# Summing part of a softmax denominator with an adding DMA instead of matmuls, and spacing out a row scatter

## The reference, cut to what matters

```
x = x + relu(normalised(adj + I) @ (layernorm(x) @ W.T))          # graph stage
h = layernorm(x)
q, k, v = projections of rmsnorm(h) with rotary positions          # 4 query heads, 2 key heads, 32 channels each
att = softmax(causal(q @ k.T / sqrt(32)))                          # over 8192 positions
h = h + (att @ v) @ wo.T
out = sum over the 2 best of 8 experts of  weight * (silu(f @ w1.T) * (f @ w3.T)) @ w2.T,  f = rmsnorm(h)
x = x + h + out
```

## Time and profile before

| | us |
|---|---|
| median of 3 runs | 4111.01 (4106.96 to 4114.44) |
| the profiled execution, its own time | 4112.9 |
| its span | 4111.2 |
| attention stage in it: first to last exponential | 1496.2 to 3666.8 |

### The profile page before, as it was taken

One profiled execution on the slowest core, in us unless ns is written; L12 is line 12 of the kernel. 1 busy time (PEld: TensorE's weight loads), 2 busy tenths in 40 slices (PEclk: granted clock), 3 DMA queues, 4 the chain that ended last, 5 costly groups with the idle time before them and its releaser, 6 DMA issues. The chain is left out here.

```text
span 4111.2 us, 48117 instructions
## 1 busy us (share of the span) xinstructions
PE 3444.4 (84%) x16381; PEld 1321.4 (32%) x16381; DVE 2755.8 (67%) x3882; ACT 1306.3 (32%) x1635; POOL 1641.3 (40%) x1016
## 2 busy tenths in 40 slices
PE   1456899999999959988899899999889999965990
PEld 1233444444444422222222222222222222213650
DVE  7877887704444447777878877777777776515773
ACT  0000000000000013443454355454445455634660
POOL 1000000000000014544675496565558566873564
PEclk8567889999999969999999999999899999987995
DMA  9888998788887526500000000000000000002226
GB/s 377 345 344 345 348 336 328 290 300 303 285 298 282 206 101 243 209 10 4 26 19 6 5 24 13 10 1 10 1 17 15 6 1 6 6 16 85 72 69 210
DMA packets 165282, 572.71 MB, mean 139 GB/s; under 512 B 20193, under 2 KB 55786, under 8 KB 114550
## 3 DMA queue, kind: packets, MB, share of 16 engines
q1 hardware_dynamic: 91304, 457.35, 29.8%
q10 hardware_dynamic: 60432, 88.88, 6.1%
q0 software_dynamic: 13360, 24.03, 1.8%
HBM read 478.22 MB, written 90.57 MB: 138 GB/s over the span
## 5 line engine op out<-in xcount | busy, mean ns | idle before, releaser
L958 DVE TENSOR_REDUCE unit_max<-ps_max 128x1 f32<-128x512 f32 (+3 forms) x2176 | 1356.3, 662 | 422.8 <-PE ps_max L1215 306.7
L786 POOL TENSOR_TENSOR chunk_sum<-chunk_sum,probs 128x1024 f32<-128x1024 f32 (+1 forms) x528 | 1194.8, 2263 | 570.2 <-ACT probs L918 556.1
L918 ACT ACTIVATE probs<-ps_scores 128x1024 f32<-128x1024 f32 (+1 forms) x1088 | 1021.1, 984 | 1048.3 <-PE ps_scores L1234 858.8
L1215 PE MATMUL ps_max<-keep_k_stack,q_stack 96*128 96x512 f16 (+3 forms) x2176 | 762.7, 383 | 154.0 <-DVE unit_max L958 113.9
L1234 PE MATMUL ps_scores<-q_stack,keep_k_stack 97*128 97x512 f16 (+3 forms) x2176 | 617.3, 379 | 38.6 <-ACT probs L918 34.7
L1245 PE MATMUL ps_out<-probs,keep_v 128*32 128x512 f32 (+3 forms) x4352 | 567.1, 593 | 0.6 <-ACT probs L918 0.6
L314 DVE TENSOR_TENSOR partial_degree<-partial_degree,ring 128x2048 f32<-128x2048 f32 x240 | 550.0, 2292 | 7.1
L1215 PEld LDWEIGHTS ps_max<-keep_k_stack,q_stack 96*128 96x128 f16 x2176 | 182.1, 97 | 972.3 <-DVE unit_max L958 822.1
L497 PE MATMUL ps_gather<-ring,keep_attended 128*128 128x512 f32 x960 | 448.2, 629 | 22.1 <-DVE keep_attended L338 22.1
L512 PE MATMUL ps_gather_low<-ring,keep_attended 128*128 128x512 f32 x800 | 360.6, 607 | 1.4 <-DVE keep_attended L338 1.4
L277 POOL DMA_DIRECT2D scratch_lower<-lower x15 | 9.3, 618 | 815.3 <-ACT lower L416 815.3
(11 more groups left out here) (232 smaller groups left out, 2712.2 us busy)
## 6 DMA issues: line engine op xcount, KB each, us to landing
ring<-in_adj SPq DMA_DIRECT2D x392, 1024.0 KB, 7.0
scratch_slots<-empty_rows ACTq DMA_DIRECT2D x16, 2080.0 KB, 7.4
scratch_parts<-empty_part ACTq DMA_DIRECT2D x8, 2048.0 KB, 7.7
moe_parts<-scratch_parts SPq DMA_DIRECT2D x64, 256.0 KB, 4.8
moe_x_rows<-scratch_slots SPq DMA_DIRECT2D x39, 260.0 KB
x_in<-in_x SPq DMA_DIRECT2D x16, 256.0 KB, 7.0
x_in<-in_x ACTq DMA_DIRECT2D x16, 256.0 KB, 9.8
cos<-in_cos ACTq DMA_DIRECT2D x16, 256.0 KB, 7.2
```

What stands on the lines that cost most here:

```text
L786: nc.gpsimd.tensor_tensor(chunk_sum[:, :, lo:], chunk_sum[:, :, lo:], weights, ALU.add).then_inc(chunk_added, 1)
L918: nc.scalar.activation(probs[:, j, kv, :, lo:], ps_scores[kv][:, :, lo:], ACT.Exp, scale=SCALE).then_inc(exp_done, 1)
L958: nc.vector.tensor_reduce(unit_max[:, i, at:at + 1], bank[:, 0:width], AX_X, ALU.max).then_inc(bank_free, 1)
L1215: last = nc.tensor.matmul(out[:, 0:width], q_stack[0:SHIFT_ROW, T % QBUF, h, s * P:(s + 1) * P], k_stack[0:SHIFT_ROW, h // NREP, G * BT:G ...
```

## The change

In the units with 1 <= v < T (105 of the 136), key head 1 of chunks 0 and 1 is no longer summed by PE. After adding chunk 1 of key head 0, POOL issues one DMA over `probs[:, 0:2, 1]` (128 partitions x 2 chunks x 1024 float32, 1 MB) into a new SBUF tile `unit_sums` of that shape: a plain copy in the first such unit of a block, an adding DMA (`accum_op=ADD`) in the others. ACT waits for that DMA before it overwrites key head 1 of chunks 0 and 1 in the next unit. Once per block with T > 1, in the last chunk of unit v = T, PE contracts `unit_sums` with the ones, as `add_weights` does. Without the pair after j = 1, PE keeps the gap order of the even chunks in chunk 1. Separately, `scattering` spreads the scatters (and the copies on ACT that go with them) of the batches with pace 2, the first three, over every second chunk: 16 units instead of 8.

```diff
+    first_added = {}
+    for T in range(NB):
+        for v in range(1, T):
+            first_added[first_unit(T) + v] = v == 1
+    added_before = lambda unit: sum(1 for other in first_added if other < unit)
...
         for b, start in enumerate(scattered_at):
-            n = (unit - start) * SUB + j
-            if 0 <= n < len(batches[b]) * SUB * TOPK:
+            n, late = divmod((unit - start) * SUB + j, paces[b])
+            if 0 <= n < len(batches[b]) * SUB * TOPK and not late:
                 yield b, n
...
+        unit_sums = sb("unit_sums", [P, 2, NREP, BT])
...
+            def add_pair(T, unit):
+
+                pool.wait_ge(exp_done, unit * EXPS + PER_CHUNK * 2)
+                if added_before(unit):
+                    pool.wait_ge(pair_added, 16 * added_before(unit))
+                out, src = (tile.rearrange("p c r t -> p c (r t)") for tile in (unit_sums[:], probs[:, 0:2, 1]))
+                if first_added[unit]:
+                    if T > 2:
+                        pool.wait_ge(unit_sums_used, T - 2)
+                    pool.dma_start(out, src).then_inc(pair_added, 16)
+                else:
+                    pool.dma_start(out, src, accum_op=ALU.add).then_inc(pair_added, 16)
...
                         add_chunk(T, first_unit(T) + n, j, n == 0)
+                        if first_unit(T) + n in first_added and j == 1:
+                            add_pair(T, first_unit(T) + n)
                         route(first_unit(T) + n, j)
...
                         if kv == 0:
                             act.wait_ge(chunk_added, unit * SUB + (j - SUB + 1))
+                        elif unit - 1 in first_added and j < 2:
+                            act.wait_ge(pair_added, 16 * added_before(unit))
...
+            def add_unit_sums(T):
+
+                pe.wait_ge(pair_added, 16 * added_before(first_unit(T) + T))
+                for half in range(2):
+                    for r in range(NREP):
+                        at = half * NREP + r
+                        last = nc.tensor.matmul(ps_sum[at * HD:(at + 1) * HD, :], keep["ones_heads"][:],
+                                                unit_sums[:, half, r, :], start=False, stop=True, skip_group_check=True)
+                last.then_inc(unit_sums_used, 1)
...
                 for j in range(SUB):
-                    paired = not diagonal and j % 2
+                    by_dma = unit in first_added and j < 2
+                    paired = not diagonal and j % 2 and not by_dma
...
-                    weigh(G, j, diagonal)
+                    last = weigh(G, j, diagonal)
+                    if by_dma:
+                        last.then_inc(chunk_used, 1)
...
-                    if j in ((2, 3) if diagonal else (1, 3)):
+                    if v == T and T > 1 and j == 3:
+                        add_unit_sums(T)
+                    if j in ((2, 3) if diagonal else (1, 3)) and not by_dma:
                         add_weights(j if j % 2 else j - 1, diagonal).then_inc(chunk_used, 2)
```

More of the change, by code:

```diff
@@ L704, in attention_stage @@
         chunk_added = sem("chunk_added")
+        pair_added = sem("pair_added")
+        unit_sums_used = sem("unit_sums_used")
         numerator_copied = sem("numerator_copied")
```

## The result

| | before | changed |
|---|---|---|
| median of 4 runs each | 4109.8 us (4107.0 to 4114.4) | 4166.2 us (4164.7 to 4169.2) |
| ratio | | 1.0136, 95% interval 1.0117 to 1.0155 |
| profiled execution's span | 4111.2 | 4167.6 |

The change makes the kernel 56 us slower. The forecast was 17 us faster. The rival of a slow DMA names 4174 us, but for a landing after 9.0 us; the landing took 8.1 us, so that this number came out near the measured one is luck.

What follows compares the result with a forecast made beforehand. PE was taken to bound block 14 and POOL block 15, with DVE next in line. Gains of 19, 10 and 34 less 10, 4 and 32 gave 17 us, so 4095 us, own range 4080 to 4105.

Steps and rivals of the forecast that it cites:

- rival of a slow DMA: Cycle through probs replaces the matmuls as bound, shown at ACT's wait; 4174 us for landing after 9.0 us; chance 0.27.
- D = 7.2: just hidden in plain units.: D, from start of POOL's issue to the adding DMA's landing, is 7.2 us; hidden in plain units below 7.7.
- Plain: 13.55 becomes 12.48.: In units without preparing or routing, blocks 3 to 14, losing one add_weights shortens 13.55 us to 12.48.
- 53 x 0.65 = 34 us.: The 53 preparing, routing or first units outside block 15 gain 0.65 us each, bounds 0 and 1.07.
- add_unit_sums: -10.: PE's eight added passes at block ends cost 0.8 us in 13 blocks, hidden at the turn to block 15.
- Early fills: -4.: In blocks 2 to 4 the pair shares DMA engines with 2 MB fills; 4 us lost, 18 at worst.
- Block 15: -32.: POOL is the bound: 8 us lost in seven units without scatters, 23 in six with, 1 in the last.
- Scatters at half pace: 13.05.: About 20 plain units beside scatters go to 13.05 us of POOL work, saving 0.5 us instead of 1.07.
- even out: Rival: landing after 7.6 to 8.1 us, block 15 takes back the gain, within 8 us of 4111; chance 0.13.
- quick DMA: Rival: landing after about 5 us, block 15 costs 16; 4074 us, or 4060 with mixed units' full gain; chance 0.18.
- D = 10: Slow-DMA case, landing after 10 us: +1 on 38 units more and 50 or so in block 15; 4230 us.
- dear issue: Rival: the issue costs POOL 2 us; block 15 pays 13 more, scatter stretches return to 14.0; about 4118; chance 0.08.

Runs made afterwards that it cites:

- e6: Changed kernel with every pair DMA a plain copy instead of an addition; 4107.8 us, timed once.
- e4: Changed kernel without any pair DMA, ACT's wait for it and add_unit_sums, nothing summed in their place; 4068.3 us, ratio to the kernel before 0.9877.
- e9: The e4 kernel with DVE reading only 256 of 512 columns of each maxima tile outside the diagonal; 3949.5 us, timed once.
- e1: Changed kernel with block 15 left as before, 91 adding units instead of 105; 4114.6 us, ratio to the kernel before 0.9994.
- e7: Changed kernel without pairs in the six units of block 15 that scatter (128 to 133); 4121.3 us, timed once.
- e8: Changed kernel with the pairs issued by SP instead of POOL, as plain copies; 4083.5 us, timed once.
- e2: Kernel before with only the half pace of the first three batches' scatters; 4119.2 us, ratio 1.0007.
- e3: Changed kernel with the scatters at full pace in all batches; 4261.9 us, ratio to the kernel before 1.0353.

## Why the prediction was wrong, by its own steps

**"D = 7.2: just hidden in plain units."** D is 8.1. A 4 KB packet of the addition holds an engine 370 ns in the mean (median 361), against 179 (median 167) for one of e6's copies, so a pair needs 16 x 0.37 = 5.9 us of data instead of the 5.0 that I took from the best slice of the graph stage; what is left, 2.2 us, agrees with my 2.1 from the scatter. The mis-sized term is the data. The formula of the Trainium skill's page "DMA: Bandwidth & Descriptors" ("Anatomy of one DMA - SWDGE (gpsimd) path") gave 6.8 with both reads: 1.3 us short here, and 4.4 for the copy, 1.0 short. In spite of it the DMA was hidden in most plain units, since these went to 13.06 and not to 12.48, and the limit of 7.7 moved up by the same 0.6; eight of the 38 took longer, 7 us in sum, which e4 and e6 do not have.

**"Plain: 13.55 becomes 12.48."** This step failed most plainly, and its reason is shown. I took the 2.84 us of a chunk between two long ones as its own length. It is 2.84 only because the long neighbour takes over a reduction; alone it is 3.15 (DVE rows above, e4), and with shorter reductions 12.53 a unit come back (e9). DVE's 2.65 us for four reductions was read as a bound that overlaps with PE; in a lone chunk 0.63 us of waiting for PE come on top of it. 38 units gained 11 us, not 29. The row that said so was in my hands: 0.63 us of DVE waiting for PE in every chunk, although DVE had less work than the chunk was long.

**"53 x 0.65 = 34 us."** This is the term with the largest miss: the 53 units gained nothing in sum. The 33 preparing and first units gained 18, 0.54 each. The 20 routing units lost 17.6 (e1 16.8, e7 only 7.9) where 13 of gain were counted. I had used, the small copy held for 2.37 us, to discount a gain, and had not asked what holds it: POOL, which gets an instruction more. The sign is what I missed, since I bounded the class from below at 0. The clock was no term at all, though after such a wait PE's passes took 1.94 instead of 1.06 us (e8's section).

**"add_unit_sums: -10."** -17 in 14 last units. The matmuls cost 0.86 in each quiet one, as taken (21.94 against 21.08 us). Of the rest e6 gives 9 us back: it goes with the length of the addition. At the turn to block 15 the shift DMA hid the matmuls, as the prediction said (20.99 against 20.95 us).

**"Early fills: -4."** They have no class of their own. The one pair that took 11.8 us was issued at 1666.9, beside the fills, ACT waited 4.6 us for it, and the last unit of block 3 took 26.6 instead of 23.0 us (29.2 in e7); these 3.6 are in the 17 above.

**"Block 15: -32."** -51. Beside scatters 5.5 a unit instead of 3.8: the wait of 4.1 instead of 2.7 and an issue of 1.3 with 0.3 behind it instead of 1.05. The eight others cost 18 (e7) instead of 9, in three units and not evenly. The mechanism (scatter stuck behind the pair in one queue, ACT at the gate) was right: the term was mis-sized. The single queue that the prediction cites from the Trainium skill agrees with the 4.1 us, which fell to 1.4 behind a copy (e6).

**"Scatters at half pace: 13.05."** Most plain units take 13.06, with scatters and without, and six of the eight longer ones lie beside scatters, 5.8 us in sum. That my 13.05 for POOL's work equals this 13.06 is luck: it is PE's and DVE's turns that make it (e4). Alone the pacing is neutral (e2), beside the pairs it saves some 89 us (e3); I had not priced its absence.

In sum the 63 us of gain in blocks 2 to 14 became 11 + 18 - 18 = 11, and the 46 of loss became 17 + 51 + 1 (diagonal units) = 69: 58 slower. D = 8.1 lay at the edge of "even out", so the rival's price for it was wrong too: the terms beside D failed.

Three prices of rivals do not follow from their own terms. The quick DMA with the full gain of the 53 units is 37 + 53 x 0.42 = 59 us under 4111, 4052 and not 4060. D = 10 "and 50 or so in block 15" would be 4262; 4230 needs 18 there. The dear issue, with 14.0 in the scatter stretches, gives 4126, and its 4118 counts them at 13.55. None of these enters the forecast of 4095.

## What to carry to other kernels

A step's length read between two unlike neighbours isn't its length when it stands among its own kind: look for the engine that waits a fixed time in each step before counting the removed work as gained. Work handed from a full engine to a DMA issued by POOL is paid in POOL's queue: a scatter issued behind it lands after it, and POOL's wait for that scatter becomes a wait for the transfer; and DVE's small operations wait for POOL. Put such a transfer only where POOL has nothing that waits for a landing, and outside stretches with many small DVE operations; chosen in this way it brought 0.4%. Before a difference of a few us in one class of one profile is explained, look at the same class in two profiles with the same program there.

## What the runs showed of the hardware

- An adding SBUF-to-SBUF DMA of 1 MB lands 8.1 us after its issue and occupies POOL 1.2 us; a plain one 5.4 us and 0.76 us. The time per 4 KB packet is 361 against 167 ns (medians; means 370 and 179, the copies those of e6): an addition takes the engines slightly more than twice as long as a copy.
- Issued by SP, the same copies cost nothing in routing units beside the kernel without them (e8 against e4: 352.8 and 357.1 us) and 5 us in block 15 (196.9 and 191.6), where POOL's copies cost 20.
- The row of a POOL add right behind such an issue begins up to 0.4 us before the issue's row ends and lasts 2.79 us; counted from the issue's end it is the usual 2.37.
- After PE had waited 4.22 us for DVE, and 7.65 us for ACT, its eight float32 passes took 1.94 us at 1.2 GHz instead of 1.06 at 2.4.
- In block 14 PE was busy 212.4 of 218.6 us before the change, at full clock, and still each 1.07 us of PE work taken away shortened a plain unit by only 0.49: DVE and PE alternate over two banks.
